# Attention's head: the first two units' tiles are transferred one by one from three queues, and unit 0's values start three halves behind

## The reference, cut to what matters

```python
x = x + 0.5 * ffn(layernorm(x))      # mixture of 8 experts, top 2, plus a shared expert
x = x + attention(layernorm(x))
x = x + 0.5 * ffn(layernorm(x))

# attention, 4096 tokens of width 128, one head, 4096 memory keys and values, all fp32
q = h @ Wq.T + bq
scores = q @ memory_keys.T / sqrt(128)
probs = softmax(scores)
out = (probs @ memory_values) @ Wo.T + bo
```

## Time and profile before

| | |
|---|---|
| median of 3 runs | 657.42 us (654.88 to 660.15) |
| the profiled execution | 654.31 us |
| its span in the trace | 652.5 us |
| TensorE busy, share of the span | 93% |
| VectorE / ScalarE / GpSimd busy | 81% / 70% / 60% |
| granted TensorE clock, mean | 0.991 of full |
| SP's queue / ScalarE's queue, share of the 16 DMA engines | 34.6% / 2.8% |

### The profile page before, as it was taken

How to read it: one execution, slowest core, us unless ns; L and a number is a source line. 1 busy time by engine, 2 the same in 40 slices (tenths; PEclk the granted TensorE clock), 3 DMA queues, 4 the chain that set the end, 5 groups by cost and what they waited for, 6 DMA issues and landing times.

```text
span 652.5 us, 9360 instructions
## 1 busy us (share of the span) xinstructions
PE 609.1 (93%) x2868; PEld 432.8 (66%) x2884; DVE 526.0 (81%) x944; ACT 455.4 (70%) x765; POOL 390.0 (60%) x427
## 2 busy tenths in 40 slices
PE   7799998579889999999999999999999988999997
PEld 3455544467677877877777777787787767645543
DVE  4989876858978878888897897887888857699885
ACT  3577786266667768777677776777776774667886
POOL 4987670053466866767677586596677786524100
PEclk9999999979999999999999999999999998999999
DMA  8021210225374473643735727437365360000000
GB/s 309 5 64 34 66 32 1 63 66 117 85 175 92 115 158 81 149 107 87 175 85 130 153 61 175 106 90 168 73 147 119 76 130 1 1 17 17 33 32 33
DMA packets 35600, 59.18 MB, mean 91 GB/s; under 512 B 8544, under 2 KB 9184, under 8 KB 35424
## 3 DMA queue, kind: packets, MB, share of 16 engines
q1 hardware_dynamic: 31936, 53.87, 34.6%
q10 hardware_dynamic: 3616, 4.73, 2.8%
HBM read 8.23 MB, written 2.10 MB: 16 GB/s over the span
## 4 chain that ended last, share of the span: by engine, by line
PE 66%; DVE 21%; issue 4%; ACT 4%; SPq 1%; DMA 1%; ACTq 1%; POOL 1%; DVEq 0%; POOLq 0%
PE banks L1348 7%; PE banks L1389 7%; PE banks L1391 7%; PE banks L1390 7%; PE banks L1349 7%; PE banks L1350 7%; PE banks L1368 5%; DVE bank_max L1071 4%; DVE E L1066 4%; DVE probsT L967 4%; PE banks L1209 4%; PE banks L1200 3%; PE banks L1399 2%; PE banks L1222 1%; SPq L337 1%
## 5 line engine op out<-in xcount | busy, mean ns | idle before, releaser
L522 POOL TENSOR_TENSOR p_lo<-probsT,p_hi 128x768 fp32r<-128x768 f32 (+1 forms) x128 | 226.9, 1776 | 161.5 <-ACT p_hi L717 160.7
L1071 DVE TENSOR_REDUCE bank_max<-banks 128x1 f32<-128x1024 f32 x128 | 156.1, 1220 | 35.4 <-PE banks L1350 34.4
L717 ACT ACTIVATE p_hi<-probsT 128x768 fp32r<-128x768 f32 (+1 forms) x128 | 104.5, 816 | 26.7 <-PE banks L1391 23.6
L1348 PE MATMUL banks<-kv_lo,q_parts 128*128 128x512 f32 x256 | 112.2, 438 | 7.2 <-ACT E L735 4.7
L1066 DVE STREAM_TRANSPOSE E<-E 128x1024 f32<-128x1024 f32 x92 | 113.5, 1234 | 1.7 <-ACT E L735 1.7
L967 DVE SCALAR_TENSOR_TENSOR probsT<-banks,E 128x1024 bf16<-128x1024 f32 x80 | 95.3, 1217 | 20.1 <-PE banks L1200 19.9
L624 ACT ACTIVATE probsT<-probsT 128x1024 bf16<-128x1024 bf16 x96 | 92.5, 982 | 23.7 <-DVE probsT L967 18.5
L735 ACT ACTIVATE E<-banks,neg_max 128x1024 f32<-128x1024 f32 x92 | 102.3, 1112 | 8.9 <-DVE neg_max L1077 5.1
L1389 PE MATMUL banks<-p_hi,kv_lo 128*128 128x512 f32 x256 | 108.2, 423 | 0.0
L1390 PE MATMUL banks<-p_lo,kv_hi 128*128 128x512 f32 x256 | 102.8, 402 | 0.0
L1391 PE MATMUL banks<-p_hi,kv_hi 128*128 128x512 f32 x256 | 102.8, 401 | 0.0
(11 more groups left out here) (127 smaller groups left out, 884.9 us busy)
## 6 DMA issues: line engine op xcount, KB each, us to landing
probsT<-E SPq DMA_DIRECT2D x248, 128.0 KB, 2.4
probsT<-E SPq DMA_DIRECT2D x168, 64.0 KB, 2.0
E<-in_keys_values SPq DMA_DIRECT2D x8, 512.0 KB, 3.4
probsT<-E ACTq DMA_DIRECT2D x56, 64.0 KB, 2.4
out<-X SPq DMA_DIRECT2D x8, 256.0 KB, 2.0
X<-in_x SPq DMA_DIRECT2D x1, 1280.0 KB, 9.0
probsT<-E ACTq DMA_DIRECT2D x8, 128.0 KB, 4.1
X<-in_x SPq DMA_DIRECT2D x3, 256.0 KB, 5.2
```

Source lines behind the costliest of these rows:

```text
L522: pool.tensor_tensor(moved_part(p_lo, ring), moved_pair(ring // UP, ring % UP), moved_part(p_hi, ring).bitcast(fp32), ALU.subtract).then_i ...
L717: act.activation(moved_part(p_hi, ring), moved_pair(ring // UP, ring % UP), ACT.Copy).then_inc(moved_hi_done, 1)
L1071: dve.tensor_reduce(bank_max[:, i % 2, h:h + 1], score_pair(u, i, h).rearrange("p b n -> p (b n)"), AX.X, ALU.max).then_inc(bank_max_done, 1)
L1348: pe.matmul(bank, qh, kl, start=True, stop=False)
```

## The change

- Unit 0: a tile's strips are issued as soon as this tile's squares are done, at 64 KB each. SP issues row blocks 0 and 1 of both tiles (16 DMAs), GpSimd row blocks 2 and 3 (16 DMAs, each with a semaphore of its own). ScalarE issues none.
- ScalarE waits for GpSimd's first 8 after the exponential of H = 6, and for its last 8 before `moved_high(0)`.
- `FIRST_LAG` is 3: pairs 0 to 7 of unit 0 are due one half later (TensorE at H = 11 to 18). `moved_high(0)` stands at H = 8, right in front of `moved_high(1)`; `copy_oT(0)` stands at H = 17. Pair 8 stays at H = 22.
- Unit 1: its tiles 0, 1, 2 lie in the places 2, 0, 1 of `E2`, so its first tile need not wait until unit 0's are out. Each tile is transferred by itself: 12 DMAs of 64 KB from SP and 4 from ScalarE, the latter after the exponentials of H = 12, 14 and 16. From unit 2 on the batches are those of before.

```diff
-FIRST_LAG = 2
+FIRST_LAG = 3
...
-        moved = [sem(f"moved{k}") for k in range(len(BATCHES))]
+        moved = [sem(f"moved{k}") for k in range(len(BATCHES) + 1)]
+        moved_first = [sem(f"moved_first{k}") for k in range(QUADS * QUADS)]
...
+        def slot_of(u, i):
+            return (2, 0, 1)[i] if u == 1 else i
...
+        def strip(u, tile, count, b, i):
+            slot = slot_of(u, tile)
...
+        def second_batch(tile):
+            return (1, 2, 0)[tile]
+
+        def move_strip(eng, u, k, tile, count, b, i):
+            eng.dma_start(*strip(u, tile, count, b, i)).then_inc(moved[k], 16)
...
-            return w if H % HALVES == (FIRST_LAG if w == 0 else LAG) + 1 else None
+            return w if H % HALVES == (FIRST_LAG if w == 0 else LAG + 1) else None
...
     SP
+                    for tile in range(moved_tiles(0)):
+                        sp.wait_ge(squares_done, 2 * (tile + 1))
+                        for b in range(QUADS // 2):
+                            for i in range(QUADS):
+                                move_strip(sp, 0, 0, tile, 1, b, i)
+                    continue
                 wait(sp, moved_lo_done, UP * (u - 1))
+                if u == 1:
+                    for tile in range(MOVED):
+                        sp.wait_ge(squares_done, squares_of(1) + 2 * (tile + 1))
+                        for b in range(QUADS - 1):
+                            for i in range(QUADS):
+                                move_strip(sp, 1, second_batch(tile), tile, 1, b, i)
+                    continue
...
     GpSimd, before its loop over the units
+            pool.wait_ge(z_done, GROUPS)
+            pool.wait_ge(down_done, GROUPS * SLOTS)
+            for tile in range(moved_tiles(0)):
+                pool.wait_ge(squares_done, 2 * (tile + 1))
+                for b in range(QUADS // 2, QUADS):
+                    for i in range(QUADS):
+                        done = moved_first[(tile * 2 + b - QUADS // 2) * QUADS + i]
+                        pool.dma_start(*strip(0, tile, 1, b, i)).then_inc(done, 16)
...
     ScalarE, moved_high
+                if ring == UP:
+                    act.wait_ge(moved[2], 16 * QUADS * QUADS)
+                if ring == 0:
+                    for done in moved_first[QUADS * QUADS // 2:]:
+                        act.wait_ge(done, 16)
...
     ScalarE, exponentials
-                    wait(act, moved[batch_of(i)], moves(batch_of(i), u))
-                    if u == 1 and i == MOVED - 1:
+                    batch = batch_of(slot_of(u, i))
+                    if u == 2 and i == 0:
+                        act.wait_ge(moved[2], 16 * QUADS * QUADS)
+                    else:
+                        wait(act, moved[batch], moves(batch, u))
+                    if u == 1 and i == 0:
                         act.wait_ge(kv_lo_done, KV)
...
     ScalarE, loop over the halves
-                    if w is not None:
+                    if w:
                         copy_oT(w)
+                    if projection_at(H + 2) == 0:
+                        copy_oT(0)
...
-                    if u == 0 and h == 5:
-                        act.wait_ge(z_done, GROUPS)
-                        act.wait_ge(down_done, GROUPS * SLOTS)
-                        act.wait_ge(squares_done, squares_of(1))
-                        for b in range(QUADS // 2, QUADS):
-                            for i in range(QUADS):
-                                move_strip(act, 0, 0, b, i)
-                    if 0 < u < LAST and h == HALVES - 1:
+                    if u == 0 and h == 6:
+                        for done in moved_first[:QUADS * QUADS // 2]:
+                            act.wait_ge(done, 16)
+                    if H in (HALVES + 4, HALVES + 6, HALVES + 8):
+                        tile = (H - HALVES - 4) // 2
+                        act.wait_ge(squares_done, squares_of(1) + 2 * (tile + 1))
+                        for i in range(QUADS):
+                            move_strip(act, 1, second_batch(tile), tile, 1, QUADS - 1, i)
+                    if 1 < u < LAST and h == HALVES - 1:
...
                     ring = pair_at(H + 4)
-                    if ring is not None:
+                    if ring == 1:
+                        moved_high(0)
+                    if ring:
                         moved_high(ring)
```

More of the change, by code:

```diff
@@ L327, in squares_of, with batch_of @@
             return 2 * sum(moved_tiles(w) for w in range(units))
-        def batch_of(i):
-            return [k for k, (first, count) in enumerate(BATCHES) if first <= i < first + count][0]
-        def move_strip(eng, u, k, b, i):
-            first, count = BATCHES[k]
-            target = probsT[b * SQ:(b + 1) * SQ, u % 2, :, :, :].rearrange(
-                "p (t i) c q -> p i t (c q)", t=MOVED)[:, i, first:first + count, :]
-            eng.dma_start(target, E2[i * SQ:(i + 1) * SQ, first:first + count, b, :]).then_inc(moved[k], 16)
+        def slot_of(u, i):
+            return (2, 0, 1)[i] if u == 1 else i
+        def batch_of(slot):
+            return [k for k, (first, count) in enumerate(BATCHES) if first <= slot < first + count][0]
+        def strip(u, tile, count, b, i):
+            slot = slot_of(u, tile)
+            target = probsT[b * SQ:(b + 1) * SQ, u % 2, :, :, :].rearrange(
+                "p (t i) c q -> p i t (c q)", t=MOVED)[:, i, tile:tile + count, :]
+            return target, E2[i * SQ:(i + 1) * SQ, slot:slot + count, b, :]
+        def second_batch(tile):
+            return (1, 2, 0)[tile]
+        def move_strip(eng, u, k, tile, count, b, i):
+            eng.dma_start(*strip(u, tile, count, b, i)).then_inc(moved[k], 16)
         def pairs_until(H):
@@ L386, in _ @@
                     sp.wait_ge(squares_done, squares_of(u) + 2 * (first + count))
-                    for b in range(QUADS // 2 if u == 0 else QUADS - k):
+                    for b in range(QUADS - k):
                         for i in range(QUADS):
-                            move_strip(sp, u, k, b, i)
+                            move_strip(sp, u, k, first, count, b, i)
             for g in range(GROUPS):
@@ L729, in exponentials @@
                 if i < MOVED and h == 0:
-                    wait(act, moved[batch_of(i)], moves(batch_of(i), u))
-                    if u == 1 and i == MOVED - 1:
+                    batch = batch_of(slot_of(u, i))
[4 more added lines that the diff above has]
+                    if u == 1 and i == 0:
                         act.wait_ge(kv_lo_done, KV)
                 if i < moved_tiles(u):
-                    strips = E2[:, i, :, :].rearrange("p b (c q) -> p c b q", q=SQ)
+                    strips = E2[:, slot_of(u, i), :, :].rearrange("p b (c q) -> p c b q", q=SQ)
                     act.activation(
@@ L807, in _ @@
                         for i in range(QUADS):
-                            move_strip(act, u, 1, QUADS - 1, i)
+                            move_strip(act, u, 1, MOVED - 1, 1, QUADS - 1, i)
                     if prepares and h == Q_HALF - 2:
@@ L1064, in transpose_squares @@
                 dve.wait_ge(exp_done, 2 * (u * GT + i) + h + 1)
-                half = E2[:, i, :, h * N // 2:(h + 1) * N // 2]
+                half = E2[:, slot_of(u, i), :, h * N // 2:(h + 1) * N // 2]
                 dve.transpose(half, half).then_inc(squares_done, 1)
```

## The result

| | median | range | runs |
|---|---|---|---|
| before | 656.83 us | 654.88 to 660.15 | 5 |
| after | 651.84 us | 651.52 to 654.36 | 5 |

What follows compares the result with a forecast made beforehand. The prediction saw the attention's head held by unit 0's strip issues and data, TensorE idle 6.6 us. It summed +0.6 - 2.5 + 2.4 + 0.6 = +1.1 us, so 658.5 us on the median; range 650.0 to 665.0.

Steps and rivals of the forecast that it cites:

- The price of an issue on GpSimd: Unit 0's sixteen GpSimd strips: 1.05 us per issue, bounded by 0.60 and 1.34, so values start at 140.7, +0.6 us.
- rival B: GpSimd issues nearly as fast as SP, below 0.8 us; clock kept; -5.3 to -7.4 us, 650 to 652; chance 0.20.
- The clock: TensorE, idle 6.1 us before the first values, then runs them 5 us at about half clock: +2.4 us.
- The half saved: After unit 0's values, one half less remains of the stretch in which VectorE leads: -2.5 us.
- From pair 0 to the end of pair 7: Unit 0's eight pairs of values: the same 26.0 us of work as before, pair for pair and score for score.
- covered: ScalarE's 2.5 us of unit 1 strip issues at H = 14 cost nothing; H = 12 and 16 together +0.6 us.
- The strips of unit 1 in time: SP's 36 strips land 28.7 us after the first values, before the exponential of H = 18 needs them at 31.3.
- Rival D: Unit 1's strips are late: SP's issues take 1.12 us, all land 14.3 us too late, 673 us; chance 0.07.
- Rival E: VectorE's transposes in SBUF hold up GpSimd's issue during unit 0's strips: +3.6 us, 661; chance 0.06.
- Gives nothing back: From unit 2 on, strips go as before; the chain moves with unit 2's own squares, so no gain is lost.

Runs made afterwards that it cites:

- e9: The changed kernel itself, without any edit, measured a second time: 651.97 us, ratio 0.9928 to the kernel before.
- e4: The changed kernel with a copy on GpSimd between its strips of unit 0, to slow issues to about 1.05 us: 658.7 us, ratio 1.0033.
- e3: The changed kernel with unit 0's strips issued as before, 8 of 128 KB each by SP and ScalarE: 660.25 us, ratio 1.0066.
- e12: The kernel before, with ScalarE's 8 strips of unit 0 (128 KB) issued by GpSimd after both tiles' squares: 656.64 us, ratio 1.0008.
- e6: The changed kernel, but SP and GpSimd issue unit 0's strips only when both tiles' squares are done: 655.09 us, ratio 0.9982.
- e2: The changed kernel with unit 0's own tile 2 written into a place of probsT that unit 1's tile 2 uses later: 650.74 us, ratio 0.9913.
- e5: The changed kernel with unit 1's 12 ScalarE strips issued by GpSimd instead: 649.92 us, ratio 0.9899.
- e7: The changed kernel with unit 1's tiles in places 0, 1, 2 as in the kernel before: 652.31 us, ratio 0.9939.

## Why the prediction was wrong

**The price of an issue on GpSimd (failed, and decisive).** The forecast took 1.05 us, from a median of ScalarE's queue while the data held it up, and from the length of one of GpSimd's own instructions. Neither is a row of the thing priced. It measured 0.50 us, below the lower bound of 0.60 that the forecast had from a free queue. The rival B had the mechanism with less than its right chance, 0.20. In B the scores of H = 11 bound the values, at -5.5, and it was -4.4 (after) and -5.0 (e9). In after no strip is waited for: `moved_high(0)` starts without a wait, and the scores of H = 11 end at 135.99, 0.27 us ahead of the first value. e4 put the price back and got the forecast's world. The forecast's own sum for 0.60 us was -7.4; with the quick issue it misses by about 3, nearly all of it in the pairs (below). That the time lies inside the range is therefore in part luck: the issue was taken too dear and the pairs too cheap.

**The clock (the mechanism right, the term void).** +2.4 hung on 6.1 us without work. In after there was at most 1.35 from 121 us on up to the values, and the values ran at the full clock, so it was 0. In e3, e4 and e12, with 5.3 to 7.2 us, the low clock came. But rival B's condition, that under 3 us the clock is kept, does not hold: it fell to 0.68 after gaps of 1.87 and 1.81 us in e6, and to 0.81 after 2.20 in after. In e4, where it falls on the values, it cost 1.4 us (`pairs` 30.35 against 28.93), not 2.4: of its first 5 us only a part was at the lower level.

**The half saved (right).** -2.5 forecast, -2.25 measured: `rest` is 9.12 to 9.15 in all kernels with the third half of lag, and 11.39 to 11.41 in all without.

**From pair 0 to the end of pair 7 (failed).** "The work is the same 26.0 us, pair for pair", and the strips at H = 14 "covered", +0.6 in all. `pairs` went from 26.1 to 29.1, +3.0. The busy time is nearly the same (26.48 against 26.03), so most of it is waiting. What the step missed is a wait written for another purpose: the own tile of unit 1 reuses a place, and the transposes that free it were moved by the change. I had priced the later lag by the work that it moves and not by who waits for that work. "Covered" was reckoned from ScalarE's mean load, 16.0 of 26.2 us, but strips stood between two exponentials that had already been pushed together. e2 took the place's wait away and e5 the strips, and each shortened the stretch.

**The strips of unit 1 in time (right).** Rival D did not come: no exponential of H = 16 or 18 waited for a DMA.

**Rival E (did not come).** In after GpSimd issued from 120.67 to 124.88 at 0.50 us apiece while VectorE transposed from 121.04 to 122.26:

```profile
121.04 1.22 DVE L1118 STREAM_TRANSPOSE E<-E 128x1024 f32<-128x1024 f32 x1
```

**"Gives nothing back" from unit 2 on (failed in part).** The chain moves with the squares of unit 2, but SP's strips took longer in after, one of them 1.74 us, and TensorE's gap there grew from 1.65 to 2.66 us, with a clock of 0.89 behind it where before has 1.00. Of the 4.5 us that e9 is ahead at `strips`, 3.8 are left at the exponential of H = 24 and 2.3 at the maximum of H = 28. The last 1.5 us are the clock's: e5 and e7, with gaps of 2.41 and 2.29 us there but the full clock, lose nothing in that stretch (6.01 us, as in before).

**The sum by what was measured**, on after's trace: values -4.4, the pairs +3.0, the half -2.25, so -3.6 at `strips`; +2.5 up to the maximum of H = 28 and +0.6 to the end leave -0.5, and the later start of the attention by 0.6 makes the span equal to before's. On e9's: -5.0 + 2.8 - 2.25 = -4.5, and -2.7 at the end. The medians say -4.2 and -4.7 by their ratios; before's profiled execution, 654.31, was itself 2.5 under its median of 656.83, and had the full clock in all three stretches of the table.

One reading of the prediction does not come out: 16 x 128 KB in 8.3 us are 253 GB/s, not the 239 of the earlier trace rows. Nothing in its sum rests on that.

The Trainium skill's page "DMA: Bandwidth & Descriptors", section "Issuing engines are not separate DMA queues", says that another issuer saves only the issuing engine's time. Rows and runs agree with the fact (e12: the same bytes, the same landing) and not with the weight that I gave it: at the same start that time was worth 0.8% (e6 against e3), since the engine set free was the one that TensorE waited for. The same page's section "Specifications" gives the path through GpSimd a later first byte, 1 us against 0.6. For these strips of 64 KB it is not to be seen: issue to landing took 2.5 us in the median from GpSimd and 2.6 from SP.

## What to carry to other kernels

When DMAs move to another engine, the price of one issue there can decide, as it did here, and a trace without such a row doesn't give it: with such an unknown, forecast from both ends, and give the low end its full weight. An issue from an engine whose own work is not waited for is free; one from an engine that feeds TensorE can cost up to its length, even where this engine is 60% busy on average (e5). Taking it away gains nothing while another wait stands right behind it (e12). When work is moved later in a program, list every wait on its semaphore, above all those that guard the reuse of a place, and not only the readers of its result.

## What the runs showed of the hardware

- An issue from GpSimd (64 KB, SBUF to SBUF) took 0.50 us, less than one of SP (0.59). In e12, with 128 KB each, SP's went up to 0.94 in the median and 1.68 at most, while GpSimd's stayed at 0.53. The traffic is seen at the landing of GpSimd's strips there, 3.2 to 5.8 us after the issue, where the 64 KB of after took 2.0 to 2.8.
- The same idle time on TensorE costs clock in one execution and not in the next: 2.20 us at 118 to 120 us, then a clock of 0.81 in after and 1.00 in e9 and before. In 16.3 to 32.6 us, in code that is the same, it was 0.90 in after and 1.00 in both others; and after 2.35 to 2.41 us at the start of unit 3 it was 0.89 in e9 and 1.00 in e5. What decides it these traces don't show. The spans of after and e9, one kernel, differ by 2.9 us, of which at least 1.3 go with it (0.69 and 0.65), so where an edit moves 0.6%, the times of one execution are read against marks inside it, not against its end.
